# A dequantised down projection: three matmul terms with tokens on partitions, or two terms with whole-number weights and output columns on partitions

## The reference

```python
x = hidden_states                                   # (2, 1024, 512): 2048 tokens, 512 columns
xn = layernorm(x)
s = attention(xn) @ Wout.T                          # 32 heads of 16, ALiBi, causal
gate = silu(xn @ dequantize(gate_w, gate_s, gate_z))   # 512 -> 1792
up = xn @ dequantize(up_w, up_s, up_z)                 # 512 -> 1792
g = silu((gate * up) @ dequantize(down_w, down_s, down_z))   # 1792 -> 512
return x + s * g
# dequantize(w, s, z) = (w - z) * s; w and z are whole numbers 0..15,
# z and s are the same for each 128 rows of w
```

## Time and profile before

| | us |
|---|---|
| median of 3 runs | 1150.07 (1148.31 to 1150.79) |
| the profiled execution | 1146.97 |
| its span, first to last instruction | 1145.1 |
| PE, DVE, ACT, POOL busy | 1077.1, 876.7, 663.8, 368.6 |
| mean granted TensorE clock | 0.994 |

### The profile page before, as it was taken

How to read it: one execution, slowest core, us unless ns; L and a number is a source line. 1 busy time by engine, 2 the same in 40 slices (tenths; PEclk the granted TensorE clock), 3 DMA queues, 4 the chain that set the end, 5 groups by cost and what they waited for, 6 DMA issues and landing times. The chain is left out here.

```text
span 1145.1 us, 18720 instructions
## 1 busy us (share of the span) xinstructions
PE 1077.1 (94%) x6401; PEld 676.6 (59%) x6401; DVE 876.7 (77%) x2083; ACT 663.8 (58%) x1061; POOL 368.6 (32%) x474
## 2 busy tenths in 40 slices
PE   5999988999999999999999998999999999999997
PEld 4788764433333333333333333788888888887885
DVE  6788897888887887888788782677867876777776
ACT  3666556666666676676767667544544454445443
POOL 2666635121211221121122112133424433343343
PEclk9999999999999999999999999999999999999999
DMA  6255753453445436343444512100110020012001
GB/s 209 77 154 154 200 131 124 123 134 87 114 105 155 106 93 143 84 133 83 144 107 118 125 51 87 37 1 10 58 45 1 19 93 1 1 37 74 1 1 38
DMA packets 99663, 98.95 MB, mean 86 GB/s; under 512 B 28144, under 2 KB 81008, under 8 KB 99568
## 3 DMA queue, kind: packets, MB, share of 16 engines
q1 hardware_dynamic: 97936, 97.36, 31.1%
q10 hardware_dynamic: 1632, 0.39, 0.2%
HBM read 76.09 MB, written 21.23 MB: 85 GB/s over the span
## 5 line engine op out<-in xcount | busy, mean ns | idle before, releaser
L893 ACT ACTIVATE pr<-pair 128x1024 f32<-128x1024 f32 (+3 forms) x384 | 293.2, 811 | 151.5 <-PE pair L1010 97.0
L268 DVE CUSTOM_DVE_ANT_0 bank<-bank,sg 128x384 f32<-128x384 f32 (+1 forms) x488 | 227.6, 522 | 65.7 <-PE bank L278 62.7
L1270 DVE SCALAR_TENSOR_TENSOR gate<-pair,sgu,gate 128x512 f32<-128x512 f32 x168 | 126.1, 751 | 94.9 <-PE pair L1349 94.9
L1348 PE MATMUL pair<-xc_lo,w_gu 128*128 128x512 f32 x448 | 175.6, 392 | 1.5 <-DVE xc_lo L1253 1.5
L1349 PE MATMUL pair<-xc_hi,w_gu 128*128 128x512 f32 x448 | 174.7, 390 | 0.0
L271 DVE TENSOR_REDUCE mx<-bank 128x1 f32<-128x512 f32 x240 | 150.2, 683 | 8.9 <-PE bank L278 8.2
L1140 POOL TENSOR_TENSOR h_lo<-gate,h_hi 128x512 fp32r<-128x512 f32 x56 | 72.5, 1294 | 241.8 <-ACT h_hi L1165 241.8
L1190 ACT ACTIVATE gate<-gate 128x512 f32<-128x512 f32 x56 | 35.5, 634 | 168.5 <-DVE gate L1270 168.5
L278 PE MATMUL bank<-ks,qs 108*128 108x512 bf16 (+3 forms) x384 | 107.7, 329 | 5.4 <-DVE mx L268 5.1
L278 PE MATMUL bank<-xin_c,s_sb 108*128 108x512 bf16 (+3 forms) x344 | 97.5, 332 | 4.6 <-DVE mx L268 4.3
L1005 PE MATMUL pair<-s_sb,xin_c 111*128 111x512 bf16 (+3 forms) x384 | 94.4, 330 | 7.8 <-ACT dt L396 2.9
(11 more groups left out here) (116 smaller groups left out, 1955.5 us busy)
## 6 DMA issues: line engine op xcount, KB each, us to landing
stk<-parts SPq DMA_DIRECT2D x16, 768.0 KB, 5.6
zst<-in_z_all SPq DMA_DIRECT2D x24, 448.0 KB, 4.2
xin_c<-in_x SPq DMA_DIRECT2D x32, 256.0 KB, 3.0
sst<-in_w_all SPq DMA_DIRECT2D x16, 448.0 KB, 6.0
s_sb<-stk SPq DMA_DIRECT2D x96, 64.0 KB
xin_c<-stk SPq DMA_DIRECT2D x96, 64.0 KB
qs<-stk SPq DMA_DIRECT2D x96, 64.0 KB
ks<-stk SPq DMA_DIRECT2D x96, 64.0 KB
```

What stands on the lines that cost most here:

```text
L268: dve.tensor_tensor_reduce(out=src, in0=src, in1=tri[:, 512 - w:512], scale=1.0, scalar=-3.0e38, op0=ALU.add, op1=ALU.max, accum_out=dst). ...
L893: act.activation(pr[e % 3][:, 2 * p:2 * p + 2, 0:w], pair[p][:, :, 0:w], ACT.Exp, scale=SCALE)\
L1270: dve.scalar_tensor_tensor(out=a, in0=GB[j % 4], scalar=scale_of(n, k, it), in1=a, op0=ALU.mult, op1=ALU.add)\
L1348: pe.matmul(GB[j % 4], w, xc_lo[:, k, :], start=True, stop=False)
```

## The change

**Operand order.** The down product is turned round. The weights w - z, whole numbers, are the stationary operand, and h (128 inner x 512 tokens) moves. One `down(b, it, t)` now gives 128 output columns x 512 tokens, t counts tiles of output columns, and there are two terms (h_lo and h_hi) where there were three. The weights aren't split any more: `w_high`, `w_low` and their tiles are gone, and so are the multiplication and the load of the scales in the attention stage.

**Scales.** A scale now belongs to a partition of the result, and it is another one for each tile `it`, so that PSUM can't add over `it`. Each `down(b, it, t)` starts its bank anew, and the bank is read out for every `it`: for `it` = 0 and t = 0..3 by ScalarE (scaled, straight to the sum `yt[t]`); for `it` = 1..12 and t = 0, 1, 2 by ScalarE to one of three `tmp` tiles, which GpSimd adds to `yt[t]`; for t = 3, and for all four t of `it` = 13, by VectorE in one SCALAR_TENSOR_TENSOR (bank x scale + yt). The scales come by one small DMA and one transpose.

**Turning back.** y is now turned, so four groups of transposes (`trans_y`) bring it back. For all blocks but the last they stand in slot 0 of the next block, and silu, `mul_y`, `add_x` and the store follow there.

**Order.** `trans_o` and `s_project` begin one slot later. `down(1)` moves into slot 3. ScalarE's two `first` now stand ahead of `silu(it-1)`. VectorE's `gate(it-1)` stands behind a2, a3 and (from slot 4) the new reading of y[3].

```diff
 gpsimd, weight job
-                    pool.tensor_tensor(w, w, zst[:, :], ALU.subtract).then_inc(z_sub, 1)
-                    pool.wait_ge(z_sub, ip + 1)
-                    pool.tensor_tensor(w, w, sst[:, :], ALU.mult).then_inc(w_ready, 1)
+                    pool.tensor_tensor(w_half(ip, n), sst[:, :], zst[:, :], ALU.subtract).then_inc(w_ready, 1)
...
+        def reader(it, t):
+
+            if it == 0:
+                return FIRST_DOWN
+            return BY_VECTOR if it == IT - 1 or t == 3 else BY_COPY
...
 gpsimd
+                def add_down(b, it, t):
+
+                    if reader(it, t) != BY_COPY:
+                        return
+                    n = count((BY_COPY,), b, it, t) - 1
+                    pool.wait_ge(dn_copy, count((FIRST_DOWN, BY_COPY), b, it, t))
+                    summed(pool, b, it - 1, t)
+                    pool.tensor_tensor(yt[t][:, :], yt[t][:, :], tmp[n % 3], ALU.add).then_inc(dn_pool, 1)
...
+                for b in range(NB):
+                    for it in range(1, IT + 1):
+                        if it == 1 and b > 0:
+                            add_x(b - 1, 0)
+                            add_x(b - 1, 1)
+                        if it >= 4:
+                            add_down(b, it - 2, 0)
+                        h_low(b, it - 1)
+                        if it == 1 and b > 0:
+                            add_x(b - 1, 2)
+                            add_x(b - 1, 3)
+                        for m, t in {3: ((1, 0), (1, 1), (1, 2))}.get(it, ((it - 2, 1), (it - 2, 2)) if it > 3 else ()):
+                            add_down(b, m, t)
...
 scalar
                 def first(b, it, n):
 
-                    act.wait_ge(hl_done, IT * b + it + 1)
+                    if b > 0 or it > 1:
+                        act.wait_ge(hl_done, IT * b + it - 1)
...
+                        if it < IT:
+                            first(b, it, 0)
+                            first(b, it, 1)
...
+                        elif it == 2:
+                            hi_o(b, 2)
+                            silu(b, 1)
+                            hi_o(b, 3)
+                            copy_s(b, 0)
+                            copy_s(b, 1)
+                            h_high(b, 1)
+                            copy_s(b, 2)
+                            copy_s(b, 3)
+                        elif it == 3:
+                            silu(b, 2)
+                            copy_down(b, 0, 0)
+                            copy_down(b, 0, 1)
+                            h_high(b, 2)
+                            copy_down(b, 0, 2)
+                            copy_down(b, 0, 3)
+                            for t in range(KT):
+                                copy_down(b, 1, t)
+                        else:
                             silu(b, it - 1)
+                            copy_down(b, it - 2, 0)
                             h_high(b, it - 1)
...
+                            for t in range(1, KT):
+                                copy_down(b, it - 2, t)
...
 vector
-                        if it > 0:
-                            gate(b, it - 1)
...
+                        if it == 2:
+                            lo_o(b, 2)
+                        add(b, it, 2)
+                        add(b, it, 3)
+                        if it == 1:
+                            lo_o(b, 0)
+                        elif it >= 4:
+                            sum_down(b, it - 3)
                         if it > 0:
                             gate(b, it - 1)
...
+                    sum_down(b, IT - 3)
                     gate(b, IT - 1)
+                    sum_down(b, IT - 2)
...
+                    sum_down(b, IT - 1)
...
 tensor
-                    for n, (l, r) in enumerate(terms(h_hi[it % 3][:, cols], h_lo[it % 3][:, cols], wd_hi[it % 2][:, :], wd_lo[it % 2][:, :])):
-                        mm = pe.matmul(y[t][:, :], l, r, start=(it == 0 and n == 0), stop=(it == IT - 1 and n == 2))
...
+                    else:
+                        bank_read(pe, b, it - 1, t)
+                    pe.matmul(y[t][:, :], w_down(it, t), h_lo[it % 3][:, :], start=True, stop=False)
+                    pe.matmul(y[t][:, :], w_down(it, t), h_hi[it % 3][:, :], start=False, stop=True).then_inc(dn_done, 1)
...
+                    gate_up(b, 0, 2)
+                    if b > 0:
+                        trans_y(b - 1, 0)
+                        trans_y(b - 1, 1)
```

## The result

The changed kernel takes 1172.64 us (median; 1170.92 to 1174.69) against 1149.23 us for the kernel before in the same comparison: 1.0203 times as long, 95% interval 1.0182 to 1.0224. It is slower by about 2%, as forecast (1172.5 us, 1.0195 times the median known then). The profiled execution has a span of 1170.5 us against 1145.1.

A forecast was written before the change was run, and what follows sets the result against it. FFN middle slots bound by the product's loop (6.0 us), blocked to 6.37. Block 0 2.5, two blocks 5.0 each, last 9.6, small parts 0.4: 22.5 on 1145.1, plus 1.9 and 3.1, gives 1172.5 us; range 1155 to 1186.

The forecast's parts named there:

- the 3.1 us added: Whole kernel: the median of the runs shown lay 3.1 us above the profiled execution, so 1169.5 became 1172.5 us.
- TensorE's work: FFN: down loses 50.7 us of matmuls, trans_y adds 7.2, so 43.5 us less; a middle slot is 5.44 us.
- The loop: Middle slots: D0, j2, a2, a3, reading of y[3], product, h_high, h_low, next D0 take 6.0 us.
- The blocked product: Middle slots: GpSimd's add_down keeps the product waiting, ending it 0.55 us behind; the period becomes 6.37 us.
- F: Middle slots: moment when h_low(it-2) is done and D0 and first start; VectorE reaches the product at F + 3.2.
- Rival A: Middle slots: port shared without a block, or VectorE slips in cheaper; slot 6.0, kernel 1159 us; chance 0.18.
- Rival B: Middle slots: VectorE gets the port at the second add_down's change-over; slot 5.55, kernel 1143 us; chance 0.09.
- The head: Block start to F of slot 5: TensorE alone 38.9 us, waits 5.5 more, so 44.4; block 0 41.9.
- Block 0 was to be 2.5 us shorter: First block's head: trans_y (1.8) and waits on the block before (0.7) are absent; 107.3 against 109.8 us.
- the nine equal periods: Middle of each block: nine slots of 6.37 us from F of slot 5 to F of slot 14, at 101.8 us.
- 0 (bounds 0 and -1): Attention: removing GpSimd's multiplications and the scale's loads wins 0 us, since nobody waited for them.
- What would show it: Signs: product near 1.1 us, slots 6.37, TensorE idle about 0.9 each, mostly ahead of D0, block near 110.

The follow-up runs named there:

- with the loop opened: Changed kernel with the product again first in VectorE's slot from slot 4 on, and silu ahead of both first: 1142.32 us, 0.9939 times the kernel before.
- with the ends mended: Changed kernel with product first, hi_o(2) ahead of first, block's tail reordered, and two of slot 3's copies of y ahead of first: 1131.90 us.
- the additions cut: Changed kernel with GpSimd's additions to the sums covering 16 of 512 columns: 1150.43 us.
- memsets: Changed kernel with each GpSimd addition to a sum replaced by a memset of 1320 columns of a dead buffer: 1153.20 us.
- in the old kernel with its own links: Kernel before with the product behind a2 and a3, and silu behind the two first, from slot 4 on: 1169.96 us, 1.0173 times the kernel before.
- the new tail: Changed kernel with, at a block's end, y[3]'s reading and the last product ahead of the norm, and h_low(13) and h_high(13) moved earlier: 1168.25 us.

## Why the prediction was right

**The time.** That 1172.5 was met within 0.2 us is luck. The span was forecast 2.9 us too short; the 3.1 us added to come from the profiled execution to the median were too much, since the changed kernel's profiled execution lies only 0.2 below its median. The mechanism is what the runs bear out.

**TensorE's work.** The count fits where TensorE bounds: with the loop opened, the slot fell to 5.48 us against 5.44 counted. Not all of the 43.5 us was won by any kernel: with the ends mended the time is 18.6 us below the kernel before, 13.9 of them within the FFN (411.4 against 425.3 us).

**The loop.** Counted at 6.0, measured 5.99 with the additions cut and 5.99 with memsets; in the old kernel with its own links 6.8 counted, 6.82 measured. Of the two waits for `h_low`, that of D0 decides: `first` ends 0.57 us before a2 starts (1094.95 against 1095.52). One reading of the kernel before was wrong, without a part in the sum: `h_low` is done at 1077.96 and its reader starts at 1081.35, so it had 3.4 us and not 5.

**The blocked product.** The period 6.37 was measured as 6.36, the product's end 0.55 behind GpSimd's as counted from the two samples in the earlier trace rows; the product at 1.04 rather than 1.1, since VectorE came to it at F + 3.28 rather than 3.2. Rival A (a slot of 6.0, 1159 us) falls by the lengths and ends of the products; the experiment with memsets shows that without the exclusion the slot is 6.0 indeed and the kernel takes 1153. Rival B's mechanism, the change-over, is real: with the product first, VectorE gets in exactly so and GpSimd waits. There the product had been moved ahead of two `add`s and a reading, 2 us; in the changed kernel as written it doesn't occur in the middle slots.

**The head.** In block 3 the first D0 of slot 5 follows an `h_low` that ends at 1092.93 + 1.29 = 1094.22, which is 44.4 us behind the block's start at 1049.82: 44.4 was the forecast. The wait at `s_project(2)`, counted at 1.9, is 1.72; that at `s_project(0)` 0.34 for part of 1.1. These rows show both, and GpSimd's operation:

```profile
1059.52 0.51 PE L1447 MATMUL bank<-wo_hi,of_lo 128*128 128x512 f32 x1 [0.34 <-DVE of_lo L1322]
...
1069.77 0.50 PE L1447 MATMUL bank<-wo_hi,of_lo 128*128 128x512 f32 x1 [1.72 <-DVE of_lo L1322]
```

```profile
1092.93 1.29 POOL L1157 TENSOR_TENSOR h_lo<-gate,h_hi 128x512 fp32r<-128x512 f32 x1 [1.29 <-ACT h_hi L1197]
```

**Terms that were mis-sized.** Block 0 was to be 2.5 us shorter than the others; it is as long (110.0). The step that failed is "in block 0 `trans_y` (1.8) and the waits on the block before (0.7) are absent". TensorE's j2 and j3 of slot 1 wait for VectorE's a6 and a7 of slot 0, and these aren't earlier for want of `trans_y`; I had let TensorE run ahead there. In this execution TensorE's clock also was lower at just that place (below). The two can be told apart: in the kernel with the short additions the clock was at its full level there, and block 0 is 104.0 us against 105.2 for the others. So 1.2 of the 2.5 us are really absent and were lost to the clock in this execution, and 1.3 were the failed step. The last block's `mul_y(0)` starts 11.5 us behind a7 (1151.28 to 1162.81), not 11.0; there too the clock was down, in `down(13)` (below).

Slots 11 to 13 of blocks 0 to 2 are 6.52 us, not 6.36, which the nine equal periods left out. The norm of the next x stands in VectorE's program there, and it too is lengthened beside GpSimd's additions, 1.01 us where it takes 0.54 in the kernel before; GpSimd's pair takes 2.73 and its third addition, and so the product, come 0.17 later:

```profile
912.51 1.01 DVE L1317 TENSOR_SCALAR xnc<-xin_c,xmean,xrstd 128x512 f32<-128x512 f32 x1
```

The sum by blocks is 110.03 - 104.82, 110.14 - 104.78 and 110.17 - 104.70, 4.7 for the last block up to a7 (101.46 against 96.77 us) and 5.1 from there to `mul_y(0)`: 5.2 + 5.4 + 5.5 + 4.7 + 5.1 = 25.8 us (by the unrounded values), less 0.4 by which the FFN began earlier in this execution, where the forecast had it begin 0.4 later: 25.4 on the span, as measured, against 22.5 forecast. From `mul_y(0)` to the end both take 7.7 us.

The median moved by 23.4 us only. The stages ahead of the FFN seem to have become shorter, where the forecast put the multiplications and the scales' load at 0 (bounds 0 and -1). Take each kernel's difference of medians to the kernel before, and from it the difference of their FFNs in the profiles: for the changed kernel and the seven built on it 2.4 to 5.4 us are left as won outside the FFN; for the one built on the kernel before, which keeps the multiplications, -0.6. That is an estimate, since it takes the FFN of the other executions to be as long as that of the profiled one; which of the removed parts gives it stays open. The end of the last block:

```profile
1151.28 0.74 DVE L1339 SCALAR_TENSOR_TENSOR sg<-pair,sgu,sg 128x512 f32<-128x512 f32 x1
...
1162.81 1.29 DVE L1359 TENSOR_TENSOR s_sb<-bank,s_sb 128x512 f32<-128x512 f32 x2 [1.43 <-ACT bank L1254]
```

**What would show it.** The slot, the product's ends and the block's length came out as named. TensorE's idle time in a slot is 0.9 us, but not "most ahead of D0": in the rows above it is 0.31 ahead of j0 and 0.09 ahead of j1, which wait for a4 and a5, 0.15 ahead of D0, and 0.11, 0.10 and 0.11 behind the three restarts. VectorE's late product delays a4 and a5 too. So there is a second way round, from the product by a4, a5, j0 and j1 to D0, that is only 0.15 us shorter than that by `h_low`, and the forecast didn't name it. The loop by `h_low` decides the length, but a faster `h_low` alone could win no more than this 0.15 in a slot (an estimate from these rows).

## What to carry to other kernels

A cut in the bound engine's work can be worth nothing where the same edit closes a loop between iterations: write down what iteration n + 1's first instruction needs of iteration n, and sum the links from rows, before counting the saving. Where GpSimd is filled with work that reads SBUF, look for a wait at each VectorE instruction with two SBUF operands (here the product, and the norm with one tile in SBUF too). Put it where GpSimd changes over with time to spare, or give it an operand in PSUM that nobody else needs soon. When such a change is slower, look for the place of one instruction before giving up the idea: here the place of the product, with its silu, was worth 30 us.

## What the runs showed of the hardware

- The exclusion works both ways, and a waiting VectorE gets in between two operations of GpSimd: the product 0.76 us and GpSimd's pair 3.03 instead of 2.55 in the one kernel; the product 1.04 and GpSimd's pair 2.55 in the other. Wherever in GpSimd's addition the product comes, it ends 0.54 to 0.56 us behind it: it took 0.76, 1.04 or 1.77 us. A product with one operand in PSUM doesn't take part (0.69), nor does the product beside GpSimd's memset (0.68; a memset of 1320 columns takes 1.20 us, three in a row 3.90).
- The norm (TENSOR_SCALAR, one 128x512 tile in SBUF) does wait, for the memset too: 0.54 us alone, 1.01 beside GpSimd's additions, 0.90 beside the memsets. No run tells why it differs from the product here.
- VectorE's `add` takes 0.74 to 0.75 us whether it writes SBUF or, as a7 in the kernel with one operand in PSUM, the PSUM bank that it reads (0.75).
- After the attention's end the granted clock falls for a few us, in all ten profiles, but not at the same instant. In the changed kernel's profiled execution it is 0.63 over 719 to 723 us, so part of that stretch at 1.2 GHz, just when block 0 starts; TensorE had been idle for 1.7 and 1.6 us shortly before. In the kernel before it is 1.00 there. Where it fell within block 0 (the changed kernel, the one with memsets, the one with the new tail), `h_low(0)` is done 13.1 to 13.7 us behind the block's start, in the other five built on the changed kernel 12.4.
- It falls again in the changed kernel's last `down(13)`, to 0.50 over 1157.0 to 1160.3 us, after TensorE had been idle for 3.35 us: the matmuls start 0.43 us apart instead of 0.23.

The first stretch in the changed kernel (columns: stretch, length, busy of PE, PEld, DVE, ACT, POOL, clock, DMA share, GB/s):

```profile
719.00:723.00 4.00, 3.52 (x9) 2.78 (x10) 1.32 (x3) 1.38 (x2) 0.00 (x0) 0.63 0.29 96
```
